# Linear attention with a gated delta rule and twelve experts: products shared in one bank, squares and masks on ScalarE, new step order, new ends of the experts' part

## The reference, cut to what matters

```python
def step(Sst, inp):                        # per token, 32 value heads
    q_t, k_t, v_t, g_t, beta_t = inp
    Sst = Sst * jnp.exp(g_t)[..., None, None]
    kv = jnp.einsum('bhk,bhkv->bhv', k_t, Sst)
    delta = (v_t - kv) * beta_t[..., None]
    Sst = Sst + k_t[..., None] * delta[:, :, None, :]
    o = jnp.einsum('bhk,bhkv->bhv', q_t, Sst)
    return (Sst, o)
...
xn = _rms_norm(out) * norm_w               # out: [b, s, 32, 128]
gated = jax.nn.silu(z) * xn
return gated.reshape(b_, s_, VALUE_DIM) @ W_out
...
for e in range(E):                         # 12 experts, top 3
    h = jax.nn.relu(jnp.einsum('bsh,hi->bsi', x, w1[e]) + b1[e])
    h = jnp.einsum('bsi,ih->bsh', h, w2[e]) + b2[e]
    out = out + mask[..., None] * (w_e * h)
pooled = out.mean(axis=1)
phi = jax.nn.sigmoid(jax.nn.relu(pooled @ Wp1 + bp1) @ Wp2 + bp2)
return out * (1.0 - (phi > 0.7)[:, :, None] * 0.8)
```

## Time and profile before

| | us |
|---|---|
| three runs | 1511.1, 1513.2, 1515.6 (median 1513.2) |
| the profiled execution | 1513.1 |
| its span, first to last instruction | 1511.4 |
| TensorE busy | 1422.6 (94%) |
| VectorE busy | 1129.0 (75%) |
| ScalarE busy | 1060.1 (70%) |
| GpSimd busy | 704.5 (47%) |
| granted TensorE clock, mean | 0.976 of 2.4 GHz |

### The profile page before, as it was taken

One profiled execution on the slowest core, in us unless ns is written; L12 is line 12 of the kernel. 1 busy time (PEld: TensorE's weight loads), 2 busy tenths in 40 slices (PEclk: granted clock), 3 DMA queues, 4 the chain that ended last, 5 costly groups with the idle time before them and its releaser, 6 DMA issues.

```text
span 1511.4 us, 38181 instructions
## 1 busy us (share of the span) xinstructions
PE 1422.6 (94%) x15004; PEld 1133.0 (75%) x15004; DVE 1129.0 (75%) x1992; ACT 1060.1 (70%) x2136; POOL 704.5 (47%) x619
## 2 busy tenths in 40 slices
PE   5679999999999999999999999999877999999995
PEld 3459888897888889888888888888853465665675
DVE  5579999999999999999999999998765421221224
ACT  6467887878788887878888787887646646546430
POOL 0535545455554544555545455544327534435330
PEclk9799999999999999999999999999999899999997
DMA  3000203112020211202021120302330211111100
GB/s 115 1 1 23 57 2 58 23 37 36 23 58 2 58 23 37 36 23 58 9 51 31 29 37 22 57 13 33 69 77 31 70 36 36 59 47 36 36 1 29
DMA packets 101000, 55.92 MB, mean 37 GB/s; under 512 B 74572, under 2 KB 93016, under 8 KB 100824
## 3 DMA queue, kind: packets, MB, share of 16 engines
q1 hardware_dynamic: 100824, 53.47, 14.8%
HBM read 35.62 MB, written 1.05 MB: 24 GB/s over the span
## 4 chain that ended last, share of the span: by engine, by line
PE 70%; DVE 9%; issue 7%; POOL 5%; ACT 5%; DMA 4%; DVEq 0%; SPq 0%; POOLq 0%; ACTq 0%
PE bank L387 8%; PE bank L1327 8%; PE bank L1311 7%; PE bank L542 5%; PE bank L588 4%; PE bank L559 4%; PE bank L529 3%; PE bank L577 3%; PE bank L568 3%; DVE con L878 3%; DMA sqo<-oo 3%; PE bank L469 2%; ACT h L1427 2%; PE bank L477 2%; PE bank L485 2%
## 5 line engine op out<-in xcount | busy, mean ns | idle before, releaser
L878 DVE SCALAR_TENSOR_TENSOR con<-bank,taps,con 128x1022 f32<-128x1022 f32 (+2 forms) x192 | 245.4, 1278 | 13.0 <-ACT con L657 8.4
L1633 POOL TENSOR_TENSOR h<-h 128x512 f16<-128x512 f32 x120 | 147.4, 1231 | 162.6 <-ACT h L1427 155.5
L1034 POOL TENSOR_TENSOR gl<-const_sb,gc 128x512 f16<-128x512 f32 x128 | 129.6, 1039 | 144.2 <-DVE gc L888 84.3
L387 PE MATMUL bank<-x,qkv 128*128 128x512 f16 x768 | 184.5, 392 | 10.8 <-DVE con L878 10.8
L1311 PE MATMUL bank<-y,w 128*128 128x512 f16 x720 | 170.2, 387 | 10.8 <-ACT h L1427 8.1
L1426 ACT ACTIVATE h<-bank,b 128x512 f32<-128x512 f32 x120 | 82.4, 687 | 122.0 <-PE bank L1311 120.2
L1327 PE MATMUL bank<-w,h 128*128 128x256 f16 x1440 | 162.9, 276 | 1.7 <-DVE facc L1542 1.2
L1327 PEld LDWEIGHTS bank<-w,h 128*128 128x128 f16 x1440 | 141.6, 99 | 23.5 <-DVE facc L1542 3.6
L1311 PEld LDWEIGHTS bank<-y,w 128*128 128x128 f16 x720 | 64.1, 99 | 112.1 <-ACT h L1427 47.7
L387 PEld LDWEIGHTS bank<-x,qkv 128*128 128x128 f16 x768 | 73.2, 100 | 93.3 <-issue 12.3
L936 DVE TENSOR_TENSOR X<-X,bank 128x512 f16<-128x512 f16 x192 | 129.6, 682 | 15.2 <-PE bank L477 13.4
(11 more groups left out here) (217 smaller groups left out, 3924.3 us busy)
## 6 DMA issues: line engine op xcount, KB each, us to landing
w<-in_w SPq DMA_DIRECT2D x24, 640.0 KB, 4.5
w_qkv<-in_W_qkvz SPq DMA_DIRECT2D x16, 512.0 KB, 3.9
w_z<-in_W_qkvz SPq DMA_DIRECT2D x16, 256.0 KB, 2.8
w_out<-in_W_out SPq DMA_DIRECT2D x16, 256.0 KB, 3.0
Z<-in_xT SPq DMA_DIRECT2D x2, 512.0 KB, 5.7
y<-in_x SPq DMA_DIRECT2D x1, 1024.0 KB, 8.1
sqo<-oo SPq DMA_TRANSPOSE x64, 3.1
out_dram<-y SPq DMA_DIRECT2D x8, 128.0 KB, 1.8
```

The source lines that it names most:

```text
L387: last = mm(bank[:, b], qkv16[:, w, a, t * P:(t + 1) * P], x16[:, x, a, b * S:(b + 1) * S], start=(a == k == 0), stop=(a == HT - 1 and k = ...
L878: stt(out=out, in0=bank[:, 0:B, 0:S - k], scalar=taps[:, par, t, TAPS - 1 - k:TAPS - k], in1=out, op0=ALU.mult, op1=ALU.add).then_inc(tap_ ...
L1034: last = tt(gl[:, g % 2, k].rearrange("p (m r) d -> p m r d", m=2), upper.unsqueeze(1).unsqueeze(1).broadcast_to([P, 2, R, P]), gc[:, par, ...
L1633: tt(h16[:, n % 3, 1, t, at], h32[:, k % H32], h16[:, n % 3, 0, t, at], ALU.subtract).then_inc(h_low, 1)
```

## The change

In the attention `apply_once` leaves its product in its bank and `finish_z` goes on in it, with three products; `once` has semaphores of its own in place of a bank's release. The copy of Z comes out of that bank.

The squares of the outputs are made matrix by matrix on ScalarE with a sum each (accum_out), written over the f16 buffer `oo16`, which is dead then; VectorE keeps one instruction for their scaling. `oT` gets memory of its own. The masks of the last two levels and the first chunk's copy of the state go to ScalarE, the mask as a scale of one column per piece.

ORDER and BANK are new tables; a step may now run three heads ahead (the loads and splits of the projection's weights). A special order of the first walk with work is kept under a new name.

In the experts' part the hidden rows have two buffers, TensorE runs first(0), first(1), the gate sums, second(0), the biases, and then first(n + 1) ahead of second(n). From the third expert on the first stage goes through four banks. The first tile of the first expert writes `facc`, and the biases are added. Weight splits stand in other places. At the end the sums of rows are cut in four and put in the midst of the last products, and ScalarE centres and scales the first four row blocks.

```diff
@@ tensor: apply_once, finish_z
-                last = mm(out[:, j * P:(j + 1) * P], res0[:, g, j], Z0[:, 4 * g + j], start=True, stop=True)
+                last = mm(out[:, j * P:(j + 1) * P], res0[:, g, j], Z0[:, 4 * g + j], start=(j == 0), stop=True,
+                          skip_group_check=True)
...
-            is_free(pe, n, ("res", g), ("once", g), taking=("Z", g))
-            out = take(n, "Z", g)
+            pe.wait_ge(once_ready[g], n + 1)
+            is_free(pe, n, ("res", g))
+            out = at_bank("once", g)
...
-                mm(out[:, at], res0[:, g, j], once[:, g % 2, j], start=True, stop=False)
-                mm(out[:, at], res1[:, g, j], Z0[:, u], start=False, stop=False)
-                mm(out[:, at], res0[:, g, j], Z0[:, u], start=False, stop=False)
-                last = mm(out[:, at], ident16[:], Z0[:, u], start=False, stop=True)
+                mm(out[:, at], res0[:, g, j], once[:, g % 2, j], start=False, stop=False, skip_group_check=True)
+                mm(out[:, at], res1[:, g, j], Z0[:, u], start=False, stop=False, skip_group_check=True)
+                last = mm(out[:, at], ident16[:], Z0[:, u], start=False, stop=True, skip_group_check=True)
@@ scalar: new y_level, su; square_out
+            if l < LEVELS - 2:
+                return
+            is_full(act, n, ("y", lh), ("p", (l - 1, h)))
+            pairs_of = 2 ** (LEVELS - 1 - l)
+            for q in range(pairs_of):
+                cols = slice(q * P // 2 // pairs_of, (q + 1) * P // 2 // pairs_of)
+                last = do(Y[:, h, :, cols], at_bank("y", lh).rearrange("p (u k) -> p u k", u=8)[:, :, cols], ACT.Copy,
+                          scale=ymask[:, l, cols.start:cols.start + 1])
...
-            last = do(sqo[:, c % 2], oo[:].rearrange("p (b c r) d -> p b c r d", b=B, c=CH)[:, :, c], ACT.Square)
+            for b in range(B):
+                for r in range(R):
+                    u = (b * CH + c) * R + r
+                    last = do(oo16[:, u // 4, 0, u % 4], oo[:, u], ACT.Square, accum_out=sso[:, u:u + 1])
@@ experts: banks and order on TensorE
-H_BANKS = (3, 5)
-LOGIT_BANK, SUM_BANK = 4, 6
-O_BANKS = (2, 7)
+H_BANKS = (2, 3, 0, 5)
+LOGIT_BANK, SUM_BANK = 5, 7
+O_BANKS = (6, 4)
...
-                    pe.wait_ge(h_evac, n * HK + k - 1)
+                    pe.wait_ge(h_evac, q - (3 if q >= 2 * HK + 4 else 1))
...
-        first(2, between={4: gate_sums, 8: turn_gates})
+        gate_sums()
+        second(0, between={(2, 0, IT - 1): turn_gates})
         biases()
-        for n in range(E - 3):
+        for n in range(1, E - 1):
+            first(n + 1)
             second(n)
-            first(n + 3)
-        second(E - 3)
-        second(E - 2)
...
+        second(E - 1, between={(1, 0, 3): lambda: pool_rows(0), (2, 0, 3): lambda: pool_rows(1), (2, 1, 2): lambda: pool_hidden(0),
+                               (3, 0, 0): lambda: pool_phi(0), (3, 0, 3): lambda: pool_rows(2)})
+        pool_rows(3)
@@ experts: ScalarE
+            if g == 2:
+                act.wait_ge(par_in, 128)
+                do(b2_16[:, 0], b2[:], ACT.Copy, scale=SCALE).then_inc(b2_parts, 1)
+                split2_high(act, 0)
...
-        split2_high(act, 0)
-        split1_high(act, 2)
-        first(1, between={IT - 1: chosen})
+        first(1, between={IT - 1: chosen})
+        split1_high(act, 2)
         split2_high(act, 1)
@@ experts: VectorE
+        for n in range(1, E - 1):
             gate_column(n)
-            if n + 4 < E:
-                split1_low(dve, n + 4)
             for k in range(OK):
+                if k == 0 and n + 2 < E:
+                    split1_low(dve, n + 2)
+                if k == OK - 1:
+                    split2_low(dve, n + 1)
                 second_tile(n, k)
-            split2_low(dve, n + 2)
@@ experts: the end on ScalarE
+        act.wait_ge(means_made, 1)
+        for m in range(CH):
+            do(y[:, m], y[:, m], ACT.Identity, bias=means[:, m:m + 1]).then_inc(centred, 1)
+        act.wait_ge(rstd_ready, 6)
+        for m in range(CH):
+            act.wait_ge(centred, m + 1)
+            do(y[:, m], y[:, m], ACT.Copy, scale=rstd[:, m:m + 1]).then_inc(first_mixed, 1)
```

Of the new ORDER two lines from the middle of a walk:

```diff
-    (1, "turn", (1, 1)), (1, "p", (3, 0)), (2, "gc", 0), (0, "sum", 0),
+    (2, "gc", 0), (1, "turn", (0, 1)), (0, "sqo", 2), (1, "p", (2, 0)),
```

284 lines of the change are left out of this document (158 added, 126 removed), and 68 rows, old and new, of tables (BANK, ORDER).

## The result

The changed kernel takes 1518.7 us (median of 7 runs, 1515.6 to 1523.7) where the kernel before takes 1511.1 (7 runs, 1508.0 to 1515.6): a ratio of 1.0049 with a 95% interval of 1.0028 to 1.0070. It is 0.5% slower; 1476 was forecast. The profiled execution took 1523.7 us, the longest of its seven and 5 us over their median, with a span of 1521.9.

What follows compares the result with a forecast made beforehand. TensorE's own instructions were taken to bound each head. From 1513.1 us, 13.4 (correction), 10.4 (experts' beginning), 8.1 and 2.8 (middle) and 2.3 (end) were subtracted, with moves and order at 0, giving 1476.1 us; range 1463 to 1492.

Steps and rivals of the forecast that it cites:

- What bounds the kernel: Attention heads: each is paid in TensorE's own instructions, busy 65.5 of a 65.6 us period, VectorE close behind.
- The correction, -13.4 us: Attention: three products for four drop 16 per head, 0.90 us in each of 15 heads; holding the bank longer costs nothing.
- Work moved to ScalarE, 0: Attention: VectorE loses 5.4 us per head, ScalarE gains 5.0, hidden in its idle time; neither gain nor loss.
- The new order, 0 with ends -10 and +13: Attention's new step order: effect unreadable from the trace, taken as 0 us, between 10 gained and 13 lost.
- the sign: Whole kernel against the kernel before: faster 0.94, same 0.02, slower 0.04.
- SyncE's load: Attention: loading the next head's z weights behind the third transpose was expected to cause no wait.
- The experts' beginning, -10.4: Experts' first four passes: 77.1 us become 66.7 as ScalarE's weight splits leave the gaps between stages; 10.4 us gained.
- The term of 3.0 us: Experts' beginning: loss to the half clock behind the biases, counted again within the 66.7 us.
- The middle, -10.9 in two terms: Experts' middle: four banks from the third expert on gain 8.1 us, a weight split moved on VectorE gains 2.8.
- the end, -2.3: Experts' end: row sums within the last products; last second stage to kernel end 32.4 us for 34.7, 2.3 gained.
- Rival 1: Attention: the order opens gaps that eat the products' gain, period stays 65.6 us, kernel 1489.5 us; chance 17%.
- Rival 4: Attention: ScalarE becomes each head's bound, period 70.6 us, kernel slower at 1560 us; chance 4%.

Runs made afterwards that it cites:

- newend: Kernel before with only the changed experts' part, attention's order and banks untouched: 1485.9 us, ratio 0.9853 to the kernel before.
- ocb: oc with the banks of the first su and the first pdl exchanged: 1471.9 us, ratio 0.9743 to the kernel before.
- fourth: after with the correction's fourth product computed again: 1531.8 us, ratio 1.0142 to the kernel before.
- oc: newend with the three-product correction in a shared bank, old order, new bank table: 1477.5 us, ratio 0.9789 to the kernel before.
- ocs: oc with only the squares' sums moved to ScalarE: 1485.3 us, ratio 0.9834 to the kernel before.
- ocbl: ocb with squares' sums on ScalarE, VectorE's step on them later, fourth squares behind a turn's copy: 1476.9 us, ratio 0.9773 to the kernel before.
- kdv: kd with squares' sums, last two levels' masks and first state back on VectorE: 1683.2 us, ratio 1.1141 to the kernel before.
- kd: after with GpSimd's first two decayed-key steps moved behind its third low part: 1506.7 us, ratio 0.9987 to the kernel before.
- ocbc: ocb with GpSimd's second-chunk decayed keys moved earlier and computed five times, beside VectorE's gating: 1502.4 us, ratio 0.9936 to the kernel before.
- after: The changed kernel with all parts of the change, against the kernel before: 1518.7 us, ratio 1.0049.
- ocm: oc with all three moves to ScalarE (squares' sums, masks, first state), old order: 1488.8 us, ratio 0.9870 to the kernel before.
- kdz: kd with the banks of the first z product and turn (3, 0) exchanged: 1506.5 us, ratio 0.9969 to the kernel before.
- kdy: kdz with the second decay product put behind the fifth level's first product: 1505.8 us, ratio 0.9968 to the kernel before.
- kdh: kdz with the squares' sums left out, so the output differs from the reference: 1501.9 us, ratio 0.9944 to the kernel before.

## Why the prediction was wrong, point by point

- **What bounds the kernel.** Right: the usual period went from 65.37 us to 64.35 with one product less per matrix in the old order (newend, ocb), and from 67.21 to 68.11 with one more in the new (fourth).
- **The correction, -13.4 us.** Right as a term: 13 to 14 us in the new order (fourth), 10 with my first banks (oc), 17 with better ones (ocb). That the longer hold of a bank costs nothing depends on the table: two banks exchanged were 7 us.
- **Work moved to ScalarE, 0.** Wrong, +12 us. The loads were well worked out: ScalarE 58.98 us in a period where 58.5 was said. The squares stand 0.29 us apart in ocs, not 0.25. The failed step is "what hides it is the idle time left on ScalarE, 6.2 us per period". That time lies elsewhere; at one place four squares stand ahead of a copy for which TensorE then waits 0.60 us per head, and the mean share can't tell this. One place further on the same work costs 0.1 us per head (ocbl). That VectorE's relief is worth nothing was not run by itself in the old order; in the new one it is needed (kdv).
- **The new order, 0 with ends -10 and +13.** Wrong, +27 us, and the step that turned the sign. The failed step is "I take 0 for the order, with -10 and +13 as ends". The upper end had no row behind it; it was the size of the gain beside it. What the runs showed in its place: 9 to 12 of the 27 are the meeting of VectorE's gating with GpSimd (kd; ocbc in the old order; the two kinds of heads in after). VectorE's 56.7 us per period became 60.4 in the window, of which 2.5 are the gating step at 507.20 (3.61 us for 1.13). The rows for it were there: the prediction read 2.17 us against 1.23 as this very sharing, and the order's lists told which GpSimd steps come beside `weigh`. Some 17 us remain, 1.2 per head between kd and ocm, and their cause stays open. kdz, kdy and kdh each took one named wait away and got 0 to 4 us; the waits came back under other names. I hold that the order has little room at many places at once, but this is argued, not shown; of the banks only one exchange was tried. That SyncE's load would make no one wait was right: ScalarE sat idle ahead of its split of z (L633) four times, 2.7 us in all, each time for VectorE and never for the load.
- **The experts' beginning, -10.4.** Right: 67.8 us from the first stage to the fourth pass's end (1176.26 to 1244.05) where 66.7 was said. The granted clock behind the biases was low again, 0.71 over 8 us. The prediction reads 0.60 over 8 us as half the time at 1.2 GHz; with levels of 1.2 and 2.4 GHz it is four fifths of it. The term of 3.0 us comes from a row and doesn't hang on this.
- **The middle, -10.9 in two terms, and the end, -2.3.** Right: an expert every 26.05 us (1257.15 and 1478.50 with 8.5 experts between), and the last second stage, beginning at 1478.50 + 13.1 = 1491.6, is followed by the end after 30.3 us, where 32.4 was said, 2 us better than forecast.
- **The rivals.** Rival 1 had the larger mechanism, an order that opens gaps, but let it eat no more than the 13.4 us of the products; it ate 27. Rival 4 had the right side and the right point, 1.7 us per period above 65.6; the mean period was 2.2 above, that in the window 2.6. Its mechanism, ScalarE as the bound of each head, is not what happened: ocm has the same ScalarE and a mean period of 65.6. No rival had an order that brings two engines together in one memory, and none let the order cost more than the products gained, though the prediction says that what it can lose is open.

## What to carry to other kernels

Before taking a new order at nothing, list for each VectorE instruction with two SBUF inputs what GpSimd does beside it in the new lists, and price each meeting by a row that shows one. Load moved to another engine is priced by what stands right behind it there and who waits for that, not by the engine's busy share. Where several edits come in one change, run the parts by themselves: here two of the four parts, in the old order with a table of banks of their own, made 1472 us, and all four 1519.

## What the hardware showed that was not expected

- A VectorE instruction of 128 columns with two SBUF inputs took 345 ns alone and mostly 1090 to 1342 ns beside GpSimd, one per GpSimd instruction: each of the short ones pays about the neighbour's length (1.09 to 1.3 us). Whether one instruction of 512 columns in their place would pay it only once was not run.
- Squares with a sum each stood 0.29 us apart in the attention's end (545.08, 545.37), against 0.25 in the norm of q and k.
